# A macaron transformer layer: the three-way split of the row maxima runs on GpSimd instead of VectorE

## The reference

```
x = x + 0.5 * (relu(layernorm(x) @ W1q.T + b1) @ W2q.T + b2)
x = x + attention(layernorm(x))       # 16 heads of 8 channels, rotary q and k, softmax over 512 keys
x = x + 0.5 * (relu(layernorm(x) @ W1q.T + b1) @ W2q.T + b2)
```

## Time and profile before

| | |
|---|---|
| median of 3 runs | 630.07 us (629.36 to 634.07) |
| profiled execution, first to last instruction (span) | 629.4 us; no time of its own is listed, and the lowest run is equal to it |
| TensorE matmul busy | 577.3 us, 92% |
| VectorE busy | 488.3 us, 78% |
| ScalarE busy | 365.1 us, 58% |
| GpSimd busy | 180.8 us, 29% |
| VectorE's maxima, L763 | 512 of 681 ns, 326.8 us |

### The profile page before, as it was taken

The page is one execution under the profiler, slowest core; times in us unless marked ns, Lnnn a source line. Parts: engine busy times, 40 slices in busy tenths (PEclk is TensorE's granted clock), DMA queues, the critical chain, the costliest instruction groups (busy, mean ns, idle before and its releaser), DMA issues. The chain is left out here.

```text
span 629.4 us, 11175 instructions
## 1 busy us (share of the span) xinstructions
PE 577.3 (92%) x3412; PEld 263.1 (42%) x3412; DVE 488.3 (78%) x1098; ACT 365.1 (58%) x693; POOL 180.8 (29%) x209
## 2 busy tenths in 40 slices
PE   3867979999999999999999999999999899998985
PEld 2545443423444434443535344444444234423444
DVE  6463959899888988889798979898888787887022
ACT  1211028666767675767676766667676657676822
POOL 6120008102910273006510661038102810102000
PEclk9988889999999999999999999999999989999999
DMA  7012211221121122112211212121211121100000
GB/s 232 3 38 84 74 41 59 65 76 57 43 81 54 56 67 64 41 56 71 68 59 50 76 51 76 38 72 45 85 51 67 49 72 65 56 7 1 2 18 17
DMA packets 20946, 35.96 MB, mean 57 GB/s; under 512 B 4144, under 2 KB 11824, under 8 KB 20912
## 3 DMA queue, kind: packets, MB, share of 16 engines
q1 hardware_dynamic: 20240, 35.01, 17.9%
q10 hardware_dynamic: 672, 0.52, 0.3%
HBM read 22.55 MB, written 8.39 MB: 49 GB/s over the span
## 5 line engine op out<-in xcount | busy, mean ns | idle before, releaser
L666 ACT ACTIVATE probs<-scores_T 128x512 f32<-128x512 f32 x512 | 290.8, 598 | 160.8 <-PE scores_T L492 159.8
L763 DVE TENSOR_REDUCE maxima<-scores 128x1 f32<-128x512 f32 x512 | 326.8, 681 | 58.9 <-PE scores L483 57.3
L483 PE MATMUL scores<-k_stack,q_stack 72*128 72x512 bf16 x512 | 194.6, 389 | 8.5 <-DMA k_stack<-k_scratch 4.3
L492 PE MATMUL scores_T<-q_stack,k_stack 75*128 75x512 bf16 x512 | 187.5, 384 | 8.5 <-ACT probs L666 3.8
L502 PE MATMUL heads_acc<-probs,v_heads 128*32 128x512 f32 x1024 | 136.9, 608 | 2.0 <-ACT heads L673 1.5
L483 PEld LDWEIGHTS scores<-k_stack,q_stack 72*128 72x128 bf16 x512 | 50.4, 98 | 123.0 <-DVE maxima L763 60.7
L492 PEld LDWEIGHTS scores_T<-q_stack,k_stack 75*128 75x128 bf16 x512 | 48.4, 98 | 86.5 <-ACT probs L666 57.5
L557 PEld LDWEIGHTS side<-w_q,hidden 128*128 128x128 f32 x512 | 65.7, 192 | 9.5 <-ACT hidden L656 1.4
L557 PE MATMUL side<-w_q,hidden 128*128 128x128 f32 x512 | 66.5, 275 | 1.2 <-ACT hidden L656 1.1
L566 PE MATMUL heads_acc<-ones_f 128*128 128x256 bf16 x274 | 44.9, 308 | 11.9 <-DVE thr L811 10.9
L656 ACT ACTIVATE hidden<-side,b_col 128x512 f32<-128x512 f32 x64 | 43.9, 690 | 12.0 <-PE side L551 11.7
(11 more groups left out here) (94 smaller groups left out, 494.7 us busy)
## 6 DMA issues: line engine op xcount, KB each, us to landing
q_stack<-q_scratch SPq DMA_DIRECT2D x32, 288.0 KB
k_stack<-k_scratch SPq DMA_DIRECT2D x96, 96.0 KB
k_scratch<-k_parts SPq DMA_DIRECT2D x8, 384.0 KB, 3.4
q_scratch<-q_parts SPq DMA_DIRECT2D x8, 384.0 KB, 3.4
resid<-in_x SPq DMA_DIRECT2D x8, 256.0 KB, 5.3
k_swap<-k SPq DMA_DIRECT2D x16, 128.0 KB, 2.7
q_swap<-q SPq DMA_DIRECT2D x16, 128.0 KB, 2.0
out_y<-resid SPq DMA_DIRECT2D x8, 256.0 KB, 2.0
```

Of the source, the lines that this page charges most:

```text
L483: pe.matmul(scores[:, bank_of(n, NSC), :], q_stack[0:ROWS, s, t * P:(t + 1) * P], k_stack[0:ROWS, s, :], start=True, stop=True).then_inc(s ...
L492: pe.matmul(scores_T[:, bank_of(n, NST), :], k_stack[0:ROWS + PARTS, s, t * P:(t + 1) * P], q_stack[0:ROWS + PARTS, s, :], start=True, sto ...
L666: act.activation(probs[:, s % (2 * QUAD), t, :], scores_T[:, bank_of(n, NST), :], ACT.Exp, scale=SCALE).then_inc(s_exp, 1)
L763: dve.tensor_reduce(maxima[:, c:c + 1], scores[:, bank_of(s * T + t, NSC), :], AX_X, ALU.max)\
```

## The change

The five instructions leave `max_of` on VectorE and go to GpSimd as `split_max`, with GpSimd's `tensor_scalar` by 1.0 in place of VectorE's copies. `max_of` still waits on `s_split`. The calls stand at four places of GpSimd's list, and one before it for the first quad.

```diff
-                    if c == QUAD * T - 1:
-                        split_max(i * NQ + s // QUAD)
...
+            def split_max(quad):
+
+                n = quad * SPLIT_STEPS
+                alone(pool, "pool", s_max, (quad + 1) * (QUAD * T))
+                alone(pool, "pool", s_maxT_psum, quad)
+                pool.tensor_scalar(max_parts[:, 0, :], maxima[:], 1.0, 0.0, ALU.mult, ALU.add).then_inc(s_split, 1)
+                alone(pool, "pool", s_split, n + 1)
+                pool.tensor_tensor(max_rest[:], maxima[:], max_parts[:, 0, :], ALU.subtract).then_inc(s_split, 1)
+                alone(pool, "pool", s_split, n + 2)
+                pool.tensor_scalar(max_parts[:, 1, :], max_rest[:], 1.0, 0.0, ALU.mult, ALU.add).then_inc(s_split, 1)
+                alone(pool, "pool", s_split, n + 3)
+                pool.tensor_tensor(max_rest2[:], max_rest[:], max_parts[:, 1, :], ALU.subtract).then_inc(s_split, 1)
+                alone(pool, "pool", s_split, n + 4)
+                pool.tensor_scalar(max_parts[:, 2, :], max_rest2[:], 1.0, 0.0, ALU.mult, ALU.add).then_inc(s_split, 1)
...
             inv_std("attn", 1)
+            split_max(0)
             for ph in phases(pool.Fori):
                 i = ph.i
                 if ph.core:
                     fill_values(i, 2)
                 if ph.post:
                     add_bias("out", i - 1)
+                if ph.core:
+                    split_max(i * NQ + 1)
                 if ph.ffn1:
                     inv_std("ffn1", i + 2)
                 if ph.proj:
...
                     rotate_end(pool, "pool", "k", i + 1)
                 if ph.core:
                     fill_values(i, 3)
+                    split_max(i * NQ + 2)
                 if ph.proj:
                     rotate_begin(pool, "q", i + 1)
                     rotate_end(pool, "pool", "q", i + 1)
...
                 if ph.post:
                     inv_std("ffn2", i - 1)
+                if ph.core:
+                    split_max(i * NQ + 3)
+                if ph.post:
                     add_bias("ffn2", i - 1)
                 if ph.ffn1:
                     inv_std("attn", i + 2)
+                if ph.next_max:
+                    split_max((i + 1) * NQ)
                 if ph.proj:
                     fill_values(i + 1, 0)
                     fill_values(i + 1, 1)
```

More of the change, by code:

```diff
@@ L736, in norm @@
                                         "apply_rest": range(T // 2, T)}[what])
[L738 to L751, removed]
             def max_of(head, tiles):
```

## The result

The changed kernel takes 687.18 us (median, 684.75 to 689.88) against 629.73 for the kernel before in the same runs: the ratio is 1.0885, 95% interval 1.0831 to 1.0938. The profiled execution, the longest of the four, has a span of 688.1 us, 58.7 more than before.

The account below looks back on a forecast made before the run. TensorE, full in the loop, was taken as the bound: 629.4 + 33.8 (stall) + 4.3 (hand-over) + 11.8 (clock) = 679.3, less 0.7 for small VectorE waits, 678.6; forecast 679 us, range 661 to 700.

Parts of the forecast that it names:

- The chain behind split 2: Step 4: split delays q's rotation and the DMAs behind it; TensorE stalls 4.8 us a batch, 33.8 us in all.
- its rival: TensorE's clock holds because `max_row(i, 2)` may split the stall in two: 667 us, chance 0.20.
- The split's own price: Five small instructions on GpSimd at 0.23 us each; with waits 2.28 us in the loop, 1.78 in written-out phases.
- The hand-over: Steps 0 and 12: VectorE's next first maximum waits for GpSimd; TensorE loses 0.54 us each, 4.3 us in the loop.
- within the slack of 0.36: Written-out phases: 1.88 us from one maximum to the next against 1.48, claimed to cost nothing.
- The clock: Behind each of seven stalls TensorE's granted clock falls to the 1.2 GHz level, 1.7 us each, 11.8 us.
- The twofold end: Upper bound of the clock's loss behind the seven stalls: twice the 11.8 us.
- `inv_std` covered by 0.9 us: Behind split 1, first feed-forward's `inv_std` ends at 289.98, VectorE wants it at 289.96 + 0.9; no loss.
- What VectorE could give back: Work taken from VectorE returns hardly more than TensorE's 3.4 us of waits for maxima; 0.7 us in the sum.
- The hand-over alone: Rival: `stack` 0 lands in time, no stall or clock loss, only waits between quads: 634 to 638 us, chance 0.05.
- The faster case: Rival: VectorE was the bound in bursts, so TensorE's waits for maxima go: some 624 us, chance 0.04.
- The longer split: Rival: split near the wide forms' 5.3 us, `inv_std` late at step 1 too: over 700 us, chance 0.09.

Follow-up runs that it names:

- The fill: Changed kernel with 36 constant matmuls of 256 columns ahead of TensorE's wait for the next batch's stack: 663.42 us, 1.0524 to the kernel before.
- the run with q's wait: Kernel before, all splits on VectorE, GpSimd made to wait for head 11's last maximum before rotating q: 656.57 us, 1.0424.
- the kernel before with the fill: Kernel before, all splits on VectorE, with 36 matmuls of 256 columns ahead of the wait for the next batch's stack: 658.9 us, 1.0418.

## Why the prediction came out right, and where it was off

**The chain behind split 2: right, in kind and size.** The distance from head 11's last maximum to the first scores of the next batch was forecast at 22.7 us in the loop and 22.0 elsewhere, 156.8 in the seven phases. Measured from the timelines (end of head 11's last maximum to TensorE's line) it is 21.4, 22.5, 23.4, 22.4, 21.7, 22.9 and 21.3: 155.7. Against 123.0 before that is 32.7 us of stall, where 33.8 was forecast. The pieces agree: the rotation took 7.99 us, the next two 3.71 and 8.48. Two runs show that it is this place, one by taking it out (0.7% left), one by putting it in alone (7.5%), and a third shows that the order costs without the engine (4.2% with no split on GpSimd). Two signs came otherwise than forecast. TensorE's seven waits for `k_stack` make 28.5 us and not 30 to 38, because part of the stall is taken as waits for `max_row(i, 2)`, which the prediction had disappear. So the stall was split in two, as its rival had it, and the clock fell all the same.

**The split's own price: right.** 0.20 us for a 128x16 cast and 0.22 for a subtraction, against 0.23 from the 128x4 row. The doubled 0.34 for a subtraction was not met. In the loop it is 2.08 us from the maximum's end (329.08) to the split's (331.16), where 2.28 was forecast.

**The hand-over: its sum right, partly by luck.** 4.3 us were forecast, 0.54 at step 0 and 0.54 at step 12 of each phase of the loop. The two kernels' first `scores` of each head, laid side by side, show where TensorE falls behind. These are the ones around the two steps, phase 3:

| first scores of | before | changed | behind |
|---|---|---|---|
| batch 3, head 8 (step 1) | 285.40 | 311.67 | 26.27 |
| batch 3, head 9 (step 2) | 289.52 | 315.92 | 26.40 |
| batch 3, head 10 (step 3) | 293.73 | 320.77 | 27.04 |
| batch 4, head 4 (step 13) | 335.82 | 371.85 | 36.03 |
| batch 4, head 5 (step 14) | 339.86 | 376.30 | 36.44 |

At step 0 it is 0.12 us in place of 0.54. TensorE takes the fourth tile of the head at 315.20, that is 0.27 later than in the kernel before, and catches half of that up, although it is full. At step 12 it is 0.40. Over the four phases the two make 2.1 us. Another 1.9 come at step 2, where the prediction had nothing. Together it is 3.9 us (4.3 forecast). The run with split 2 back on VectorE, 4.5 us with an interval from 2 to 7, can't tell these apart. In the written-out phases the forecast put 1.88 against 1.48 "within the slack of 0.36", which it is not by 0.04. The traces show no loss there.

**The clock: right in kind, mis-sized.** The term "7 x 1.7 = 11.8 us" is the step that was too small. The fill shows 23.8 us (22.8 by the ratios). Counted from the granted clock of stretches of 2 us, as (1 - clock) x busy time behind each stall, the first six give 2.4, 2.1, 2.6, 4.8, 6.4 and 4.9 us. Head by head TensorE falls 19.6 us further behind within three heads of these six stalls. The price came from one row of the kernel before, where TensorE had stood still for 1.0 us, and was carried over to stalls five times as long. The low clock that was expected for 3 to 4 us lasted 7 to 14, part of it in the stall. That the length of the stall is the reason is not shown: behind the wait of 2.59 us in the run with q's wait it was low for as long. The twofold end that I allowed (23.6 us) is what was measured, and so the time, 687.2, lies 8 us above the forecast of 679 and inside the range.

**`inv_std` covered by 0.9 us: right, but what meets behind it was left out.** It was ready in time, as forecast. But VectorE's pairs of `tensor_scalar` come later by the hand-over, and GpSimd's 128x512 instructions of k's rotation run beside them: in phase 3 the second pair took 2.03 us, where a pair that isn't blocked takes 0.59 and this pair took 1.59 in the kernel before. With `inv_std` back in front the first pair took 2.29 us and the second 0.61, and TensorE lost no less. In the changed kernel TensorE waited 0.4 to 0.6 us for the normed rows in each of the four phases, in the kernel before in one of them. I had asked when the result is ready and not what the next work of both engines does to each other. Which of the two engines' shifts does it stays open.

**What VectorE could give back: mis-sized.** The prediction took the 3.4 us of waits for maxima for all there was, and 0.7 us for what the stall swallows. The waits for `attn_out`, 2.6 us, were there too, one of them in the earlier trace rows, and they are gone in every kernel whose split 2 has left VectorE. In the changed kernel this and the waits for maxima are 4.0 us less than before.

By stretches of the timeline the 58.7 us lie as follows. The stalls make 32.7 us. The six stretches from a batch's first scores to head 11's last maximum of the next phase grew by 23.6 us: 19.6 behind the stalls and 3.9 at steps 0, 2 and 12. The start up to head 11 in phase 0 grew by 4.5, and the end shrank by 2.1. The 4.5 us at the start are not the change's: TensorE's clock was low there from 88 to 105 us in this execution, until 92 us in that of before. In the kernel before with the fill, whose start is that of the kernel before, it was low from 87 to 97 and from 104 to 107, and the start is 3.9 us longer as well. So the price of the clock may hold some chance, in the two profiled executions; in the medians the fill removed 23.8.

**The rivals.** The clock did not hold. The hand-over alone was the whole only where q's lateness was taken away. The faster case fell as a whole, though what it counts on exists: with split 2 alone moved and q hardly late, 2.6 us of waits go and 3.9 come, and the time is 1.0035 (0.9997 to 1.0074) of the kernel before. The longer split is excluded by the rows of 0.20 and 0.22 us.

## What to carry to other kernels

Moving a step to an idle engine moves a wait into that engine's list. Ask first what stands behind it there, and follow that to the engine that bounds the kernel: here seven instructions, a write, a read of 8.5 us, and 1 us of slack. A place inside the following work, at the point where the engine is when the input gets ready, cost 0.5% where the place ahead of it cost 8.9%. A stall of an engine that is full costs its own length, and if its clock falls more behind it, here some two thirds as much again. One row of a shorter wait was a poor price for that, so give it as a range. And look at every wait for the engine that is relieved, not only at those for the moved step's own data.

## What the runs showed of the hardware

- TensorE's granted clock fell to the 1.2 GHz level behind a wait of 1.0 us in the kernel before, and did not fall behind one of 2.23 us in phase 3 of the kernel with q's wait. The length of the wait alone doesn't tell.
- Once low behind a stall of the changed kernel, it stayed there for 4 to 13 us with TensorE fully busy. In phase 3 four whole stretches of 2 us behind the stall, each with TensorE busy throughout, were at 0.50. In the kernel with q's wait it was low for some 13 us behind a wait of 2.59 us. What decides how long is not settled here.
- With 12 matmuls of 256 columns in a stall of 4 to 5 us the clock fell behind five of seven stalls, with 36 behind none of the first six.
- VectorE's `tensor_scalar` pairs on 128x128 float32 took 0.59 us, and 1.6 to 2.3 us where they ran beside GpSimd's 128x512 instructions.
- GpSimd's 128x16 float32 instructions took 0.20 us with one input and 0.22 with two, and 0.18 to 0.20 passed between dependent ones with a gate in between.
